# Expert loop of a mixture-of-experts kernel: two PSUM banks for the expert's output, one for the turned activations, and Silu ahead of the output copy

## The reference

```python
x = x + 0.5 * ffn(layernorm(x), router_w, gate_w, up_w, down_w)
x = x + attention(layernorm(x), W_qkv, W_out)      # 16 heads of 64, rotary, causal
x = x + 0.5 * ffn(layernorm(x), router_w, gate_w, up_w, down_w)

def ffn(x, ...):                                   # E = 8 experts, top 2, F = 512
    top_vals, top_idx = top_k(x @ router_w.T, 2)
    combine = sum(one_hot(top_idx, 8) * softmax(top_vals)[..., None], axis=1)
    for e in range(8):
        y = (silu(x @ gate_w[e].T) * (x @ up_w[e].T)) @ down_w[e].T
        out = out + combine[:, e:e+1] * y
```

## Time and profile before

| | |
|---|---|
| three runs | 1485.82, 1488.47, 1488.49 us; median 1488.47 |
| profiled execution, its own time | 1478.64 us |
| its span, first to last instruction | 1476.9 us |
| around the span | 1.7 us |
| TensorE busy | 1288.9 us (87%) |
| VectorE, ScalarE, GpSimd busy | 954.9, 777.2, 783.7 us |
| mean granted TensorE clock | 0.931 of full |

### The profile page before, as it was taken

One profiled execution on the slowest core, in us unless ns is written; L12 is line 12 of the kernel. 1 busy time (PEld: TensorE's weight loads), 2 busy tenths in 40 slices (PEclk: granted clock), 3 DMA queues, 4 the chain that ended last, 5 costly groups with the idle time before them and its releaser, 6 DMA issues. The chain is left out here.

```text
span 1476.9 us, 26692 instructions
## 1 busy us (share of the span) xinstructions
PE 1288.9 (87%) x8212; PEld 933.0 (63%) x8212; DVE 954.9 (65%) x2000; ACT 777.2 (53%) x2213; POOL 783.7 (53%) x726
## 2 busy tenths in 40 slices
PE   7689999922699999999999999999998959999990
PEld 7378888821366666666666666666665728888880
DVE  6833333347388888888888888888886683332334
ACT  5644444432265556565555565655655645444452
POOL 0056666532266666666656666666664015666653
PEclk7889999965599999999999999999999689999996
DMA  8011111142111221111221112221110701111115
GB/s 285 4 37 42 44 42 44 42 123 86 43 44 44 51 51 44 44 44 44 55 47 44 44 44 48 53 45 44 44 44 15 229 8 38 44 42 44 44 37 178
DMA packets 86597, 86.68 MB, mean 59 GB/s; under 512 B 10560, under 2 KB 77120, under 8 KB 85952
## 3 DMA queue, kind: packets, MB, share of 16 engines
q1 hardware_dynamic: 73024, 63.99, 16.7%
q0 software_dynamic: 9216, 18.89, 4.3%
q10 hardware_dynamic: 4224, 2.10, 0.5%
HBM read 35.66 MB, written 15.73 MB: 35 GB/s over the span
## 5 line engine op out<-in xcount | busy, mean ns | idle before, releaser
L957 POOL TENSOR_SCALAR at_prob<-at_prob,at_rec 128x128 f32<-128x128 f32 (+3 forms) x256 | 316.3, 1240 | 282.3 <-DVE at_rec L1099 282.1
L1173 ACT ACTIVATE at_prob<-at_s,at_nb 128x128 f32<-128x128 f32 (+3 forms) x512 | 265.0, 526 | 44.3 <-DVE at_nb L1091 40.4
L703 DVE TENSOR_TENSOR f_hid<-f_b,f_silu 128x512 f32<-128x512 f32 x144 | 99.6, 692 | 257.2 <-ACT f_silu L687 131.0
L1182 ACT ACTIVATE at_probT<-at_pt 128x128 f32<-128x128 f32 (+3 forms) x256 | 105.0, 436 | 261.5 <-PE at_pt L1032 261.5
L201 POOL DMA_INDIRECT f_xb<-xn_dram,f_source x144 | 139.4, 968 | 181.8 <-DVE f_source L421 126.5
L1091 DVE TENSOR_REDUCE at_nb<-at_s 128x2 f32<-128x256 f32 (+3 forms) x256 | 208.7, 816 | 16.9 <-PE at_s L1020 16.9
L593 POOL DMA_INDIRECT ys_dram<-f_y,f_target x144 | 141.8, 985 | 135.6 <-ACT f_y L683 115.0
L1085 DVE TENSOR_TENSOR at_turned<-at_pj,at_rope 128x1024 f32<-128x1024 f32 x128 | 156.2, 1220 | 54.8 <-PE at_pj L987 49.4
L1032 PE MATMUL at_pt<-ident,at_prob 128*128 128x128 f32 x1280 | 183.8, 275 | 1.8 <-DVE at_prob L1102 1.2
L1015 PE MATMUL at_s<-at_KT,at_QT 64*128 64x128 f32 (+3 forms) x1024 | 174.7, 460 | 1.4 <-ACT at_prob L1173 1.4
L639 PE MATMUL f_b<-f_down,f_hidT 128*128 x1152 | 157.9, 280 | 20.2 <-ACT f_y L683 18.9
(11 more groups left out here) (175 smaller groups left out, 2210.8 us busy)
## 6 DMA issues: line engine op xcount, KB each, us to landing
at_QT<-at_R SPq DMA_DIRECT2D x128, 128.0 KB, 2.4
at_KT<-at_R SPq DMA_DIRECT2D x128, 128.0 KB, 2.4
f_got<-ys_dram SPq DMA_DIRECT2D x32, 256.0 KB, 4.4
f_gate<-gate_t SPq DMA_DIRECT2D x16, 256.0 KB, 4.8
f_up<-up_t SPq DMA_DIRECT2D x16, 256.0 KB, 6.4
xn_dram<-f_xn SPq DMA_DIRECT2D x16, 256.0 KB, 4.6
f_down<-down_t SPq DMA_DIRECT2D x2, 2048.0 KB, 8.2
f_xb<-xn_dram,f_source POOLq DMA_INDIRECT x144
```

Of the source, the lines that this page charges most:

```text
L957: pool.tensor_scalar(w, w, rec[:, q, 1:2], None, ALU.mult).then_inc(probB_ready, 1)
L1173: act.activation(prob[q][:, h, :], s_bank[q % 2][:, h, 0:n], ACT.Exp, bias=nb[:, q, h:h + 1], scale=1.0, accum_out=sums[:, q, h:h + 1]).th ...
```

## The change

Three edits, all in the expert loop:

- The banks: `hid_bank` goes from banks 4 and 5 to bank 4 alone, and `y_bank` from bank 7 alone to banks 5 and 7, used in turn.
- The waits that belong to them: `turn_hidden(j)` now waits for the copy of hidT of block j - 1 instead of j - 2, and `project_down(j)` for the copy of y of block j - 2 instead of j - 1.
- The order on ScalarE within a step: Silu of block j now stands ahead of the copy of y of block j - 3.

```diff
-        gate_bank, up_bank, hid_bank, x_bank, y_bank = bank[0:2], bank[2:4], bank[4:6], bank[6], bank[7]
+        gate_bank, up_bank, hid_bank, x_bank, y_bank = bank[0:2], bank[2:4], bank[4], bank[6], (bank[5], bank[7])
...
                 def turn_hidden(j, k):
                     pe.wait_ge(hid_ready, j + 1)
-                    wait(pe, hidT_ready, j - 1)
+                    wait(pe, hidT_ready, j)
                     for c in range(FC):
-                        one = pe.transpose(hid_bank[k][:, c * P:(c + 1) * P], hid[k][:, c * P:(c + 1) * P],
+                        one = pe.transpose(hid_bank[:, c * P:(c + 1) * P], hid[k][:, c * P:(c + 1) * P],
                                            ident[:, :])
...
                     pe.wait_ge(hidT_ready, j + 1)
-                    wait(pe, y_ready, j)
+                    wait(pe, y_ready, j - 1)
                     for c in range(FC):
-                        one = pe.matmul(y_bank[:, 0:P], hidT[k][:, c, :],
+                        one = pe.matmul(y_bank[k][:, 0:P], hidT[k][:, c, :],
...
-                        act.activation(hidT[k][:, :, :], hid_bank[k][:, :].rearrange("p (c q) -> p c q", q=P),
+                        act.activation(hidT[k][:, :, :], hid_bank[:, :].rearrange("p (c q) -> p c q", q=P),
                                        ACT.Copy).then_inc(hidT_ready, 1)
...
-                    if has(j, -3):
-                        act.wait_ge(y_psum, j - 2)
-
-                        b = (r + 1) % AHEAD
-                        wait(act, y_out[b], 16 * uses(j - 3, b))
-                        act.activation(y[b][:, :], y_bank[:, 0:P], ACT.Copy).then_inc(y_ready, 1)
                     if has(j, 0):
                         act.wait_ge(gu_psum, 2 * j + 1)
                         wait(act, hid_ready, j - 1)
                         act.activation(silu[k][:, :], gate_bank[k][:, :], ACT.Silu).then_inc(silu_ready, 1)
+                    if has(j, -3):
+                        act.wait_ge(y_psum, j - 2)
+
+                        b = (r + 1) % AHEAD
+                        wait(act, y_out[b], 16 * uses(j - 3, b))
+                        act.activation(y[b][:, :], y_bank[1 - k][:, 0:P], ACT.Copy).then_inc(y_ready, 1)
```

More of the change, by code:

```diff
@@ L677, in step @@
                         act.activation(xt[1 - k][:, 0, :], x_bank[:, 0:P], ACT.Copy).then_inc(xhi_ready, 1)
+                    if has(j, 0):
+                        act.wait_ge(gu_psum, 2 * j + 1)
+                        wait(act, hid_ready, j - 1)
+                        act.activation(silu[k][:, :], gate_bank[k][:, :], ACT.Silu).then_inc(silu_ready, 1)
                     if has(j, -3):
```

## The result

| | before | after |
|---|---|---|
| runs | 6: 1484.98 to 1488.49 us | 6: 1494.52 to 1504.63 us |
| median | 1486.37 us | 1500.29 us |
| profiled execution | 1478.64 us | 1499.99 us |
| its span | 1476.9 us | 1498.2 us |

The ratio of the medians is 1.0089, 95% interval 1.007 to 1.0108: the changed kernel is slower by 0.9%, some 14 us. The forecast of 1470 us had the wrong sign; the 1500 lies inside the range of 1452 to 1504, on the side of rival 1.

A forecast was written before the change was run, and what follows sets the result against it. TensorE, busy 87%, was taken to bound the kernel, stalling at the down projection for the y copy. -33.3 + 14 = -19 us from the 1488.5 median gave 1470 us; range 1452 to 1504.

The forecast's parts named there:

- rival 1: Expert loops: holds end only when TensorE stands still, so the stop moves to the transposes; slower, +26 to +58 us; chance 0.31.
- What goes: Down projection L639: with two y banks its waits for the y copy vanish, 33.3 us in two loops; lower bound 0.
- What comes back: Late updates hit the next waits, chiefly the turn of x (L613): 4 more long holds per loop, 14 us back.
- the price of 1.75: Loss per long hold at the turn of x (L613): 1.4 us of stop, 1.75 us with the restart.
- its lower sum (1514): Expert loops with one 1.5 us stop at the transposes in three steps: +26 us, 1514 us.
- its sign to decide: Slower wherever stalls that come back exceed 19 in the two loops, one in seven steps.
- One bank for the transposes: L631 waits for the previous block's hidT copy with 1.59 us of cover: 0, unless its update is held over 1.6 us.
- Silu ahead of the y copy: ScalarE order: y copy comes later but TensorE needs it two blocks off; price 0 together with two y banks.
- 0.5 us on each late copy: ScalarE: the order move alone, with one y bank, would delay each late y copy by some 0.5 us.

The follow-up runs named there:

- hid_one_bank_c5: Kernel before with one bank for the transposed activations and its earlier wait, y and order unchanged, at the 1486 level: 1486.23 us, ratio 0.9998.
- order_only_c5: Kernel before with Silu ahead of the y copy and nothing else, one y bank, at the 1486 level: 1499.01 us, ratio 1.0082.
- banks_only_c4: Changed kernel with ScalarE's old order, so banks and waits alone against before, at the 1486 level: 1490.10 us, ratio 1.0024.
- banks_paced: Banks and waits alone, old order, plus a small GpSimd memset behind each gather, at the 1486 level: 1488.52 us, ratio 1.0013 against before.

## Why the prediction was wrong

An account of the two loops at the 1486 level, from each trace. "Over" is what 2 x 70 steps take above the 2 x 197.8 us of the kernel before where nothing is late; idle is TensorE's within them; stops are those over 0.6 us; clock is half the length of the stretches at 1.2 GHz. Each row is one execution: that of before lies 7.7 us under the median of its runs, that of banks_only_c4 2.8 us over.

| | profiled us | over | idle | stops | clock |
|---|---|---|---|---|---|
| before | 1478.64 | 36.0 | 21.3 | 2 | 0 |
| hid_one_bank_c5 | 1486.33 | 42.2 | 27.1 | 12 | 0 |
| order_only_c5 | 1500.26 | 54.1 | 31.9 | 31 | 0 |
| banks_only_c4 | 1492.94 | 48.4 | 28.9 | 16 | 11.9 |
| banks_paced | 1486.45 | 43.0 | 29.2 | 19 | 5.1 |
| after | 1499.99 | 57.0 | 30.8 | 24 | 5.1 |

**What goes.** Right. The 33.3 us put on the y bank all went: L639's idle is 1.1 us, and none is ended by the copy of y.

**What comes back.** This is the step that failed, in number and in price. I took 4 more long holds in each loop, 8, at 1.75 us, 14 us; with the 2 of before that would be 17.5. There are 24 stops (21 at L631, 3 at L613), and what is over is 57.0 us, 2.4 for each. So about 53 us came back in the profiled executions (57.0 less the 3.5 that the stops of the earlier trace rows cost before), not 14, and each loop is 11.5 and 9.5 us longer, where it was to be some 10 shorter. By the medians it is 33.3 + 13.9 = 47.

The number was read from a rate of long holds, 1 in "8 or so" unstalled steps, and then halved on an argument that nothing bore out. The 8 was misread, too: in the trace of before 77 of the 140 steps of both loops take 2.84 us or less, since L639 stops TensorE in about every second step. A rate per step was the wrong thing to take. In both loops of before the long stop comes right behind two unstalled steps in a row (3.32, 2.83, 2.83 and then 4.59 us; 3.25, 2.84, 2.84, 4.57), as it would if the short stop at L639 kept the holds short. Of the price of 1.75, the 1.4 for the stop itself was a little high (the 24 stops are 26.0 us of idle, 1.1 each), and what lies around a stop was priced too low: 81 of the 140 steps take more than 2.84 us. Besides all idle time (30.8) and the clock (5.1), which such stops can drop and the short ones at L639 never did, TensorE loses 21.1 us while busy. In banks_only_c4 the clock is 11.9 of its 12.4 us over before. And holds grow past 2.9 us: 3.79 in the row above.

**Rival 1** has the outcome, near its lower sum (1514): the stop is only moved, and its sign to decide, more than 19 stops, was met with 24. GpSimd's pauses over 2 us came as well, 38 in the two stretches against 4 before. Its mechanism did not come as written. TensorE was to run until the transposes find no product hid; that wait is 3.0 us, and 20 of the 24 stops over 0.3 us at L631 had their product ready and stood for the copy of hidT, the wait that the change added. Steps of 4.3 us or more were to come every third; 8 of 140 did. Its premise, that a hold ends because TensorE stands still, is against the records of the updates themselves, which for the transposes, the turn of x and the down projection are nearly complete (418 of 432 before, 385 after). Before, the updates over 0.2 us late came in 103 bursts (updates within 0.4 us of each other counted once); 93 of these fell 1.75 to 2.25 us behind the start of a gather's issue, and in 101 TensorE was still running. In the kernel after it was running in 85 of 108, and in the others it had by then stood for as long as 1.70 us. In the stop shown that was 0.47 us (188.80 to 189.27).

**One bank for the transposes, 0.** By itself right, 1.0002 and 0.9998. In the whole change its wait is the one that ends last in all 24 cases at L631, as its condition ("a hold over 1.6 us on L631's own update makes it a stall") said; by the rows of L613, that would have stood instead, at most 0.44 us later. Two banks for y beside two for hid weren't tried, since all eight banks are taken.

**Silu ahead of the y copy, 0.** Wrong where updates are late: whole 1.0089, banks alone 1.0024, so it brings some 0.65% of the 0.9, though these two stem from different series. In the table the whole change is 8.6 us more over than the banks alone, with fewer drops of the clock; what is left after idle and clock, TensorE busy but slower on its way back, is 21.1 us against 7.6. Why it stops more often was not separated. Where nothing is late, 0 is right with two banks for y (0.9985 against 0.9983 in one series). The "0.5 us on each late copy" for one y bank had the right sign, and understated it: it costs 1.25% even where no update is late.

**The baseline.** The prediction argued from one level of the kernel as if it were the kernel's own. It said the cause of the late updates was not shown, and it is not shown now: the runs say that they need the gathers on GpSimd and a condition outside the kernel that held in some series and not in others. Where that doesn't hold, none of the 36.0 us to be won exists, and the change is worth 0.15%, at the ends of the loops.

No version here beats the kernel before at both levels. The banks alone come nearest: 0.998 to 0.999 at one, 1.0024 at the other.

## What to carry to other kernels

When a semaphore comes late for a reason outside the wait, giving that wait more room does not shorten the lateness: price the next wait in the chain at the full delay, by the longest hold in the trace, with the slower steps around it and the clock that a longer stop can cost, and not by the average of the stop removed. Short and frequent stops can be cheaper than few and long ones: here 36.0 us against 57.0. Before costing a stall, see whether the same kernel shows it in another series of launches.

## What the hardware showed that was not expected

- Where updates are in time, the copy that waits on a matmul starts 0.03 us behind the matmul's modelled end. At the 1486 level, with gathers on GpSimd, such an update is held 1.6 us in the earlier trace rows, 2.88 us in the earlier trace rows and in the stop of the kernel after, and 3.79 us in banks_only_c4. Most bursts of late updates come some 1.9 us behind the start of a gather's issue (the median before). With plain loads from SyncE in place of the gathers the updates are in time again, at a ratio of 0.9727.
- The Trainium skill's page "TensorE: Matmul & The Clock Gate", section "The cost: per-tile semaphore tail", gives some 0.06 us for one increment, as an estimate by its formula. The 0.03 us of the 1444 level is within it; the section has nothing like the 3.79 us.
- One program on one core has two levels of time, 1444 and 1486 us, 2.9% apart, in separate series, with two chips seen at both. At the upper one, where updates are late, nearly half of the semaphore records of the loops are missing (1605 against 2909).
- Stops of 1.3 us and less left the granted clock at 1.00 in the loops of before. Behind stops of 2.12 us and of 1.48 us it fell to half, and the step behind the first lost 1.64 us with TensorE never idle. Three stops of 2.19 to 2.39 us left it at 1.00. What decides between the one and the other was not tested.
